# Two convolution layers on one core: the three programs between the layers made one, and the rows shared by consecutive blocks copied on chip

## What is computed

```python
# layer 0: 3x3 convolution on quantised values
x = x + conv3x3_quantised(_gn(x), w0, b0)
# layer 1: pointwise, then a 5x5 depthwise filter made from the data itself
feat = einsum('bihw,oi->bohw', _gn(x), conv_w) + conv_b
filt = einsum('kh,bchw,lw->bckl', Ph, feat, Pw)   # 5x5 adaptive mean pool of feat
x = x + depthwise5x5(feat, filt)                  # each (image, channel) has its own filter
```

## Time and profile before

| what | value |
|---|---|
| time, median of 3 runs | 5670.4 us (5669.43 to 5674.16) |
| the profiled execution | 5670.9 us, span of its instructions 5669.2 us |
| busy share: TensorE, VectorE, ScalarE, GpSimd | 90%, 81%, 71%, 20% |
| layer 0 | 0 to 2310.4 us |
| statistics, filters, stores | 2310.4 to 2405.6 us |
| layer 1 | 2405.6 to 5669.2 us |
| mean granted TensorE clock | 0.96 of full speed |

### The profile page before, as it was taken

The page is one execution under the profiler, slowest core; times in us unless marked ns, Lnnn a source line. Parts: engine busy times, 40 slices in busy tenths (PEclk is TensorE's granted clock), DMA queues, the critical chain, the costliest instruction groups (busy, mean ns, idle before and its releaser), DMA issues.

```text
span 5669.2 us, 109907 instructions
## 1 busy us (share of the span) xinstructions
PE 5107.7 (90%) x43664; PEld 3715.5 (66%) x43848; DVE 4593.1 (81%) x5377; ACT 4025.6 (71%) x2541; POOL 1154.5 (20%) x1311
## 2 busy tenths in 40 slices
PE   1989898989898989199999899899899899899899
PEld 0434343434343434089889799889799799799798
DVE  6989898989898976588778688778688688688786
ACT  1767676767676767088778688778688688688786
POOL 0000000000000000123333233333233233233233
PEclk9999999999999999599999999999999999999999
DMA  7979797979797964499999999999999999999997
GB/s 284 372 291 395 279 406 282 405 280 398 287 383 302 371 236 201 119 190 182 189 191 188 190 181 177 197 181 186 183 189 183 199 178 180 194 187 186 199 182 120
DMA packets 829155, 1349.81 MB, mean 238 GB/s; under 512 B 60474, under 2 KB 618810, under 8 KB 751418
## 3 DMA queue, kind: packets, MB, share of 16 engines
q0 software_dynamic: 184704, 537.09, 40.7%
q1 hardware_dynamic: 618882, 617.89, 38.6%
q10 hardware_dynamic: 25024, 187.38, 10.1%
HBM read 803.24 MB, written 538.84 MB: 237 GB/s over the span
## 4 chain that ended last, share of the span: by engine, by line
PE 47%; DMA 5%; SPq 3%; DVE 1%; issue 1%; ACT 1%; ACTq 0%; POOL 0%; DVEq 0%; POOLq 0%
PE c_tps L1160 35%; DMA c_x<-out_dram 5%; PE c_cps L1139 4%; PE c_cps L1140 4%; PE c_cps L1141 4%; SPq L869 3%; DVE c_z L1087 1%; DVE c_feat L1114 0%; ACT c_z L1052 0%; ACT c_feat L1065 0%; ACT c_xr L1074 0%; ACTq L958 0%; DVE c_xr L1121 0%; POOL out_dram L1011 0%; ACTq L959 0%
## 5 line engine op out<-in xcount | busy, mean ns | idle before, releaser
L1160 PE MATMUL c_tps<-c_feat,c_tt 123*128 123x256 f16 (+1 forms) x20736 | 2402.9, 274 | 125.7 <-ACT c_xr L1074 116.7
L1160 PEld LDWEIGHTS c_tps<-c_feat,c_tt 123*128 123x128 f16 (+1 forms) x20736 | 2006.5, 98 | 395.3 <-issue 128.2
L508 PE MATMUL b_ps<-b_xq,w0main 128*128 128x512 bf16 x8984 | 1991.7, 381 | 160.0 <-ACT b_haloq L442 150.1
L508 PEld LDWEIGHTS b_ps<-b_xq,w0main 128*128 128x128 bf16 x9168 | 891.5, 97 | 1255.2 <-ACT b_haloq L442 131.1
L1011 POOL DMA_DIRECT2D out_dram<-c_xr x1152 | 1060.8, 1071 | 2272.1 <-DVE c_xr L1121 1755.0
L1052 ACT ACTIVATE c_z<-c_x,c_rs 128x976 f16<-128x976 f32 x576 | 1150.7, 1998 | 254.5 <-DMA c_x<-out_dram 170.1
L1087 DVE SCALAR_TENSOR_TENSOR c_z<-c_x,c_rs,c_z 128x976 f16<-128x976 f32 x576 | 1106.6, 1921 | 138.1 <-ACT c_z L1052 118.2
L1121 DVE TENSOR_SCALAR c_xr<-c_tps 57x1024 f32<-57x1024 f32 (+1 forms) x576 | 701.2, 1217 | 518.2 <-PE c_tps L1160 452.0
L450 ACT ACTIVATE b_q<-b_ps,q_bias 128x1024 int8<-128x1024 f32 x512 | 567.2, 1110 | 599.2 <-PE b_ps L508 554.1
L1074 ACT ACTIVATE c_xr<-c_tps 57x1024 f32<-57x1024 f32 (+1 forms) x576 | 638.5, 1109 | 424.7 <-PE c_tps L1160 399.2
L1065 ACT ACTIVATE c_feat<-c_cps 122x1024 f16<-122x1024 f32 x576 | 822.6, 1428 | 131.5 <-PE c_cps L1141 99.6
(11 more groups left out here) (140 smaller groups left out, 1399.5 us busy)
## 6 DMA issues: line engine op xcount, KB each, us to landing
out_dram<-b_x POOLq DMA_DIRECT2D x128, 2048.0 KB, 8.1
out_dram<-c_xr POOLq DMA_DIRECT2D x576, 384.0 KB, 7.7
c_x<-out_dram SPq DMA_DIRECT2D x224, 976.0 KB, 21.4
b_stream<-in_x_dram SPq DMA_DIRECT2D x168, 1024.0 KB, 9.8
b_x<-in_x_dram ACTq DMA_DIRECT2D x138, 1024.0 KB, 9.1
b_x<-in_x_dram SPq DMA_DIRECT2D x138, 1024.0 KB, 8.8
out_dram<-c_xr POOLq DMA_DIRECT2D x512, 72.0 KB, 9.0
c_tt<-table_scratch ACTq DMA_DIRECT2D x56, 576.0 KB
```

The lines of the kernel that those rows point to most:

```text
L508: last = pe.matmul(ps[:, g % 3, j, :], k.w0main[:, y, d, :, :].rearrange("p o r -> p (o r)"), row(2 * i + j + y - 1)[:, d:d + W], start=(y ...
L1160: last = pe.matmul(tps[:, s % 2, o % 4, :], tt[0:rows, o, tp, 2 * d:2 * d + 2, :].rearrange("k w m -> k (w m)"), feat[0:rows, (e * N + i) ...
```

## The change

The programs `statistics_of_x1`, `filters` and `depthwise` become one `Block`.

- `filters` becomes the class `FilterTables`. Its segment sums are 8 reductions over ranges (`bin_spans`) and 8 multiply steps in place of 40 linked steps, fewer instructions are linked, and the tables are built one lot at a time. Lot 0 comes before VectorE enters `run`, lot 1 at the end of the first group (s equal to 7, where only the pointwise part runs).
- GpSimd and not SyncE stores the tables. SyncE waits for lot 0 to be stored and then loads the tables. VectorE and ScalarE wait for the stores of lot 0 and lot 1 before they write outputs 0 and 2, since the `c_xr` buffer lies where the tables lay.
- The constants of `c_feat` are set by three memsets of GpSimd before `run` and one of VectorE at step 2 of the first group. Their pattern is now columns 1 to 256 of the 258 of each row.
- `load_block` skips the first 4 rows of every block but block 0 of an image (and the first block 1). VectorE copies them from the other slot at step 6 (`tensor_copy` of 128 x 4 x 128 float32), and ScalarE waits for `copied` before a block's first part.

```diff
+    for n, (i, r, m0, m1) in enumerate(self.spans):
+        last = dve.tensor_reduce(part[:, n, :, :], sums[:, :, m0:m1, :].rearrange("p b m l -> p b l m"), axis=AX.X, op=ALU.add)
...
 def load_block(eng, buffers, slot, x1, i, skip=0):
     lo, hi = rows_in(i)
+    lo = max(lo, skip)
...
-            load_block(eng, buffers, x_slot(e, j), x1v[e + de::2][p, :, :, :, :], i)
+            load_block(eng, buffers, x_slot(e, j), x1v[e + de::2][p, :, :, :, :], i, skip=HALO if i else 0)
...
         @block.sync
+            for j in range(2):
+                load_block(sp, buffers, j, x1v[0], j)
+            ft.wait_stored(sp, 0)
             run(sp, group)
...
         @block.gpsimd
+            for m in range(XR_SLOTS):
+                pool.dma_start(buffers.starter[0:1, m:m + 1], k.b1col[0:1, 0:1]).then_inc(stored[m], 16)
+            pool.memset(feat[96:P, 0, 0, :, 1:FP - 1], 1.0)
+            pool.memset(feat[96:P, 0, 1, :, 1:FP - 1], 0.0)
+            pool.memset(feat[96:P, 1, 0, :, 1:FP - 1], 1.0).then_inc(filled, 1)
+            pool.wait_ge(filled, 1 + START)
+            ... the two edge columns, then cleared
+            ft.store(pool, 0)
+            if ft.lots > 1:
+                ft.store(pool, 1)
...
         ScalarE, high():
+                if part == 0 and j % N:
+                    act.wait_ge(copied, count(p, e, N - 1, copies(j)) + START)
...
         ScalarE and VectorE, before the output of step (e, m):
+                        if (e, m) == (0, 0):
+                            ft.wait_stored(act, 0)
+                        if (e, m) == (0, 2) and ft.lots > 1:
+                            ft.wait_stored(act, 1)
...
         VectorE, group(), step s:
+                        if s == 6 and (j + 2 < N or another(p, e)) and j + 2 != N:
+                            dve.wait_ge(zl_done, count(p, e, STEPS * N, STEPS * (j + 1)) + START)
+                            dve.tensor_copy(xt[:, x_slot(e, j), 0:HALO, :], xt[:, x_slot(e, j + 1), ROWS_OUT:ROWS_IN, :]).then_inc(copied, 1)
...
+                    if not banded and s == 2:
+                        dve.memset(feat[96:P, 1, 1, :, 1:FP - 1], 0.0)
+                    if not banded and s == STEPS - 1 and ft.lots > 1:
+                        ft.vector_tables(dve, 1)
...
         VectorE, before run():
+            dve.wait_ge(begun, START)
+            gs.vector_means(dve, 0, own_stats)
+            dve.memset(xt[:, 0, 0:2, :], 0.0)
+            gs.vector_spread(dve, 0, own_stats)
+            gs.vector_variance(dve, 0)
+            ... memsets of z
+            gs.vector_rstd(dve, 0)
+            dve.tensor_copy(rs[:, 0:1], gs.rstd[:, 0:1]).then_inc(zero_rows, 1)
+            dve.tensor_copy(rstd[:, :], gs.rstd[:, :])
+            dve.tensor_copy(mean[:, :], ps[:, 2, 0:nb]).then_inc(kept, 1)
+            dve.wait_ge(kept, 1 + START)
+            ft.vector_pooled(dve)
+            ft.vector_tables(dve, 0)
```

More of the change, by code:

```diff
@@ L637, in _ @@
                 pool.wait_ge(x1_stored[s], nb * 2 * STORE + 16)
[L640 to L691, removed]
@@ L694, in filters, with bin_spans, __init__, bin_buffers @@
-def filters(nc, nb, k, sums, mean, rstd, table_d, bias_d):
-    lots = -(-nb // 4)
-    with ExitStack() as ctx:
+def bin_spans():
+    out = []
+    for i in range(NBINS):
+        for r in range(Q):
+            ms = [m for m in range(NSEG) if i in bins_of(r, m)]
+            if ms:
+                assert ms == list(range(ms[0], ms[-1] + 1))
+                out.append((i, r, ms[0], ms[-1] + 1))
+    return out
+class FilterTables:
+    def __init__(self, nc, ctx, k, nb, sums, mean, rstd, table_d, bias_d, ps):
+        self.k, self.nb, self.sums, self.mean, self.rstd = k, nb, sums, mean, rstd
+        self.table_d, self.bias_d, self.ps = table_d, bias_d, ps
+        self.lots = -(-nb // 4)
+        self.spans = bin_spans()
+        self.chain, self.bins_ready, self.products, self.scaled, self.tables_ready = (
+            ctx.enter_context(nc.semaphore(n)) for n in ("f_chain", "f_bins_ready", "f_products", "f_scaled", "f_tables_ready"))
+        self.stored = [ctx.enter_context(nc.semaphore(f"f_stored{lot}")) for lot in range(self.lots)]
+        self.steps = 0
+    def bin_buffers(self, nc, ctx):
+        def sb(name, shape):
+            return ctx.enter_context(nc.sbuf_tensor(name, shape, F32))
+        nb = self.nb
+        self.part = sb("f_part", [P, len(self.spans), nb, 2 * NBINS - 1])
+        self.rows = sb("f_rows", [P, nb, NBINS, 2 * NBINS - 1])
+        self.bins = sb("f_bins", [P, nb, NBINS, NBINS])
+        self.pooled = sb("f_pooled", [P, nb, NBINS * NBINS])
+        self.mr = sb("f_mr", [P, nb])
+    def table_buffers(self, nc, ctx):
@@ L720, in filters @@
[L720 to L735, removed]
@@ L826, in _ @@
[L826 to L838 removed]
+        lots = self.lots
@@ new lines, in table_buffers @@
+        self.table, self.bias_rows = [], []
+        for lot in range(lots):
+            if lot == 1:
+                sb("f_apart", [P, 128])
+            self.table.append(sb(f"f_table{lot}", [P, 2, 2, NSHIFT, PR], F16))
+            self.bias_rows.append(sb(f"f_bias_rows{lot}", [P, 3, 2, 3, 2, PR], F16))
+        self.fl = sb("f_filter", [P, lots, 25])
+        self.split = sb("f_split", [P, lots, 2, 25], F16)
+        self.bias = sb("f_bias", [P, lots])
+        self.taps = sb("f_taps", [P, lots, 5, NBINS + 2])
```

270 lines of the change are left out of this document (153 added, 117 removed).

## The result

The changed kernel takes 5600.05 us (median of 4 runs, 5597.49 to 5605.73), the kernel before 5670.8 (5669.43 to 5674.16): a ratio of 0.9877, 95% interval 0.9863 to 0.9891. The profiled execution took 5597.51 us with a span of 5595.8, which is 73.4 us less than before. It is among the fastest of its four; between the medians the gain is 70.8 us. Predicted were 5595 us and a range of 5558 to 5626.

What follows compares the result with a forecast made beforehand. TensorE bounds undisturbed blocks (42.3 us); serial preparation and late x1 loads at changes of image add time. Gains of 41.6 + 2.5 + 31.5 = 75.6 us off 5670.9 gave 5595 us, range 5558 to 5626.

Steps and rivals of the forecast that it cites:

- Preparation: Serial stage before layer 1's blocks, from 2310.4 us: first pointwise matmul at 2361.5 us, against 2410.03.
- The holds: In the preparation, GpSimd's three memsets, 6.9 us together or each unhurried, hold VectorE's small instructions until 2333.8 us.
- Sums and tables: Segment sums and lot 0's tables before the first group: 44.4 us falls to 24.0, plus 1 for GpSimd's stores.
- First group: Pointwise part of block 0, layer 1: 28.5 us plus 6.9 for VectorE's memset; first banded step at 2396.9, 41.6 earlier.
- Block 2's wait: Block 2 of the first image: its 3.61 us wait for its load goes, worth 2.5 us.
- Shorter loads: At 7 changes of image, x1 loads shorter by four rows gain 4.5 us per change, 31.5 in all.
- the rate that I took as its lowest: At a change of image, the x1 queue's share of 76 GB/s: each shorter load saves 3.45 us.
- The copy: VectorE's row copy at step 6: below 0.6 us, 1.7 if held by GpSimd, hidden behind TensorE.
- 1: Rival at the changes of image: shorter loads bring next to nothing; 5627 us, or 5618; chance 0.14.
- 2: Rival: VectorE not held in preparation (up to 18 us), or second loads at image changes 7 us sooner; 5570; chance 0.20.
- 3: Rival at output 2 or the first banded step: waits for stores cost 8 us; 5606; inside the forecast's 0.60.
- 4: Rival at step 6 of the blocks: 63 row copies delay TensorE, slower than before, 5702 us; chance 0.03.

Runs made afterwards that it cites:

- e1: Changed kernel, but every block is loaded with all its rows and VectorE copies none: 5622.33 us, ratio 0.9912.
- e4: Changed kernel with loads skipping 12 rows in place of 4, so part of layer 1's input is left out: 5551.49 us, ratio 0.9792.
- e3: Changed kernel with each table load at the changes of image cut to one row, so old tables are used: 5466.98 us, one execution.
- e2: Changed kernel with an unused VectorE reduction of 1536 elements before each row copy: 5591.62 us, one execution.
- e12: Changed kernel with the ones written by ScalarE, GpSimd's remaining memset delayed, and the first group's memset moved to GpSimd: 5592.85 us, ratio 0.9858.
- e5: Changed kernel with the ones written by ScalarE and GpSimd's remaining memset delayed until 1/std and mean are kept: 5595.14 us, ratio 0.9864.

## Why the prediction was right

The range held, the number is 5 us off, and the mechanism is the predicted one in its two main terms. That the sum is so close is in part luck: the term for block 2 had the wrong sign, the term for the shorter loads is larger than what the experiments give to them, and the preparation gained more than I took.

1. *Preparation.* Predicted: first pointwise matmul at 2361.5; measured 2357.4. The holds were right: VectorE came out at 2334.2, predicted 2334.6. Sums and tables took 21.2 us (2334.3 to 2355.5), predicted 24.0 plus 1 for GpSimd's stores. Independent instructions in a row cost less than I took (8 scaled sums in 1.71 us), and the stores held nothing that can be seen: the same bias copies (L807) took 1.39 us for lot 0 and 1.38 for lot 1. On the old clock the gain of 52.6 us up to the first pointwise matmul falls into three parts: 10.2 until the sums begin (at 2344.5 before), 23.2 in sums and tables (44.4 to 21.2 us), and 19.2 between the last bias row and the first pointwise matmul (21.1 to 1.9 us), where the table stores and the barrier stood before. e1 shows the gain of the merged program as a whole; no run takes these parts from one another.
2. *First group.* Predicted 28.5 + 6.9 us, measured 37.5: the memset was 6.88 us, a gap of 1.8 stood before it, and the first copy added about 0.3 at step 6. First banded step at 2394.9 against 2396.9: 43.6 us earlier, predicted 41.6. The tables of lot 1 cost nothing, as predicted: from 2394.9 on the chain is TensorE alone.
3. *Block 2's wait.* This term of 2.5 us was wrong. The wait of 3.61 us had cost the kernel before nothing at the end: it needs 298.1 us from the first banded step to the last block of image 0, and e4, which has no wait at this place, 298.6. And e1 shows that the earlier head would have made this load 3.9 us more of a delay if it had not been shorter. Measured: -0.6. I took a wait off the path for one on it, and I looked at the place before and not at what the faster head would meet there.
4. *Shorter loads.* Predicted 4.5 us per change and 31.5 in all; the delays fell by 30.6. e1 gives 25.5 of these to the loads, 3.6 per change. The other 5.1 lie between the kernel before and e1, which differ there in nothing that I meant to change: not explained, and no more than the 147.0 to 155.4 of the kernels that are alike there differ by. By the medians the shorter loads bring 22 us in all, block 2 with them; so 4.5 per change was too high. The mechanism holds (e3: the tables make the loads late; e4: a straight line in rows), and 3.6 is close to 3.45, which one load gets at the rate that I took as its lowest, as if one of the two late loads counted; no run takes the two apart.
5. *The copy.* 0.42 us at the median, hidden; e2 shows a margin of at least 1.75 us more.
6. *Rivals.* 1 falls by e1. 2 is not what happened: the holds were there, and the changes of image gained 3.6 to 4.4 us each, not some 7. 3 is not in the changed kernel; its wait for stores appears in e12, behind a faster head. 4 falls by e2.

What I did not see: the gain of the preparation ends where it does because a next bound stands right behind it. VectorE's chain could be 16 us shorter, the first group 8.7, both together 24.2, and the medians move by 7 us (e12, intervals overlapping), because from 2312 us the loads on one queue fill nearly all the time to block 2. The DMA share of the preparation, 0.51 before and 0.96 after, was the sign of it.

## What to carry to other kernels

When a serial stage is shortened, add up the transfers that must come before the first use after it: that sum is the floor, and engine work above it is worth something only down to there. A load that is late only at some places is worth shortening only at those, and there fewer rows paid in a straight line, while moving the table burst by a step or two brought new waits, for stores and then for the tables themselves, and made it worse. Look for waits without a releaser at the places where a hardware loop goes back; writing the loop out was worth 18 us here.

## What the runs showed of the hardware

- A VectorE tensor_scalar of 8 elements issued at 2316.18, during a GpSimd memset, did not start at the end of it (2320.4): the next memset, which stood behind on GpSimd, went first, and the small instruction ended with that one at 2327.3, 11.14 us after its issue. So a held instruction can lose more than the rest of one memset. It did not have to wait for the third, which has its start at 2327.24. During that one the copy of 1 element a partition (2327.59, 0.15 us) was not held, and the copy of 8 elements behind it took 6.55 us. In e5, without these memsets, they took 0.17 and 0.16.
- Reductions, tensor_tensor, reciprocals and memsets on VectorE were not held beside a large GpSimd memset: 8 reductions took 5.48 us beside one (e5) and 5.49 without it, tensor_tensor 0.17, a reciprocal 0.20 and three memsets 0.21 together (the changed kernel, 2315.2 to 2316.2).
- ScalarE wrote the same constants as fast as GpSimd: 13.95 us for two times 8192 float16, against 6.92 to 6.95 each, and beside it VectorE's multiplication took 0.17 us (e5).
- 6.1 MB of table rows of 12,288 bytes cost 131 us at 7 changes of image, 18.7 us for each (e3, one execution), though only a quarter of the engines' time in 120 us around a change went to them. It is in short stretches that they push the load of x1 back. In the changed kernel, while a load of x1 was under way, the table queue moved 1.46 MB from 2760 to 2770 us and the queue of x1 0.15 MB; from 2770 to 2780, with 0.02 MB of tables, the queue of x1 moved 1.22 MB.
